# Three edits to a LayerNorm, attention and expert kernel: the order in which the QKV weights are loaded and used, and the queue that stores the output

## The reference

```python
def attn(x, Wq, Wk, Wv):                       # x: 8 x 4096 x 1024, per core 4096 x 1024
    q, k, v = x @ Wq.T, x @ Wk.T, x @ Wv.T     # each W 1024 x 1024
    scores = q @ k.T / sqrt(1024)              # causal
    return softmax(mask(scores)) @ v

def ffn(x, w1, b1, w2, b2, centroids, w_route):   # 8 experts, 1024 -> 512 -> 1024
    logits = normalize(x) @ normalize(centroids).T + x @ w_route.T
    gates = softmax over the top 2 of logits, 0 elsewhere
    h = gelu(x @ w1[e] + b1[e])
    return sum over e of gates[e] * (h @ w2[e] + b2[e])

x = x + attn(layernorm(x), Wq, Wk, Wv)
x = x + ffn(layernorm(x), ...)
```

## Time and profile before

| | us |
|---|---|
| median of 2 runs | 2174.48 (2174.03 to 2174.93) |
| the profiled execution | 2177.05 |
| its span, from the first to the last instruction of the slowest core (core 2) | 2175.5 |
| the other cores' spans | 2165.4 to 2172.9 |
| TensorE busy | 1889.7 (87%) |
| VectorE, ScalarE, GpSimd busy | 636.0, 496.0, 165.4 |

### The profile page before, as it was taken

One profiled execution on the slowest core, in us unless ns is written; L12 is line 12 of the kernel. 1 busy time (PEld: TensorE's weight loads), 2 busy tenths in 40 slices (PEclk: granted clock), 3 DMA queues, 4 the chain that ended last, 5 costly groups with the idle time before them and its releaser, 6 DMA issues.

```text
span 2175.5 us, 32734 instructions; the slowest of 8 cores (2165.4 to 2175.5 us)
## 1 busy us (share of the span) xinstructions
PE 1889.7 (87%) x12322; PEld 1131.7 (52%) x12448; DVE 636.0 (29%) x1606; ACT 496.0 (23%) x1140; POOL 165.4 (8%) x193
## 2 busy tenths in 40 slices
PE   2999999656688888989927899999999999999998
PEld 1777777323243443444415566555566665556663
DVE  2232322254633516050432122222212222221220
ACT  0333333211112021203003222212222222122220
POOL 1111111011100101010120000000000000000000
PEclk8999999777899999999968999999999999999999
DMA  9222221222321203030179511111001111110100
GB/s 177 62 66 78 69 78 50 81 93 92 114 71 49 92 25 117 1 102 16 54 152 171 104 40 49 49 49 49 26 34 40 49 49 49 49 47 13 49 30 39
DMA packets 41163, 142.80 MB, mean 66 GB/s; under 512 B 4114, under 2 KB 4114, under 8 KB 37938
## 3 DMA queue, kind: packets, MB, share of 16 engines
q0 software_dynamic: 25552, 73.42, 13.7%
q1 hardware_dynamic: 15458, 67.28, 9.7%
HBM read 113.44 MB, written 50.33 MB: 75 GB/s over the span
## 4 chain that ended last, share of the span: by engine, by line
PE 76%; DVE 9%; DMA 7%; issue 5%; ACT 1%; another core or an unknown queue 1%; POOL 1%; DVEq 0%; SPq 0%; ACTq 0%; POOLq 0%
PE ph L949 22%; PE pout L860 11%; PE psc L589 11%; PE pout L858 10%; PE pqk L395 9%; PE pv L356 5%; DMA x_scr<-x2b 3%; PE pctx L639 3%; PE pctx L641 3%; DVE x2b L662 2%; DMA arena<-w1s 2%; DVE stt L665 1%; DVE xr L666 1%; DMA xbuf<-x 1%
## 5 line engine op out<-in xcount | busy, mean ns | idle before, releaser
L949 PE MATMUL ph<-ln2Tg,arena 128*128 128x256 bf16 x4096 | 489.2, 285 | 35.5 <-DMA arena<-w1s 32.2
L949 PEld LDWEIGHTS ph<-ln2Tg,arena 128*128 128x128 bf16 x4096 | 386.8, 101 | 139.7 <-issue 42.1
L969 ACT ACTIVATE hT<-ph,b_s 128x256 bf16<-128x256 f32 x512 | 242.9, 474 | 754.0 <-PE ph L949 753.9
L860 PE MATMUL pout<-arena,hT 128*128 128x512 bf16 x1024 | 389.8, 381 | 11.2 <-DMA b_s<-b 8.7
L858 PE MATMUL pout<-arena,hT 128*128 128x512 bf16 x976 | 371.6, 381 | 0.0
L589 PE MATMUL psc<-qbuf,arena 128*128 128x512 bf16 x1127 | 269.0, 400 | 38.8 <-ACT probsT L602 29.3
L978 DVE TENSOR_TENSOR hT<-hT,gbc 128x256 bf16<-128x256 bf16 x512 | 149.8, 292 | 371.9 <-ACT hT L969 371.9
L395 PE MATMUL pqk<-xlnT,wqkv 128*128 128x256 bf16 x2048 | 233.1, 275 | 15.6 <-ACT arena L413 14.5
L639 PE MATMUL pctx<-arena,probsT 128*128 128x512 bf16 x504 | 201.4, 400 | 38.8 <-DVE x2b L662 38.8
L395 PEld LDWEIGHTS pqk<-xlnT,wqkv 128*128 128x128 bf16 x2048 | 200.8, 99 | 48.5 <-issue 20.0
L641 PE MATMUL pctx<-arena,probsT 128*128 128x512 bf16 x515 | 207.9, 404 | 20.4 <-DVE x2b L662 19.0
(11 more groups left out here) (95 smaller groups left out, 1052.0 us busy)
## 6 DMA issues: line engine op xcount, KB each, us to landing
xbuf<-x SPq DMA_DIRECT2D x32, 512.0 KB, 4.0
xr<-x SPq DMA_DIRECT2D x32, 512.0 KB, 3.6
x_scr<-x2b POOLq DMA_DIRECT2D x32, 512.0 KB, 3.7
x2g<-x_scr SPq DMA_DIRECT2D x16, 1024.0 KB, 5.8
out<-outsb POOLq DMA_DIRECT2D x32, 512.0 KB, 2.9
qt_scr<-qstage POOLq DMA_DIRECT2D x16, 512.0 KB, 3.8
qbuf<-qt_scr SPq DMA_DIRECT2D x8, 1024.0 KB, 6.9
ln2t_scr<-ln2Ts POOLq DMA_DIRECT2D x32, 256.0 KB, 3.2
```

The lines of the kernel that those rows point to most:

```text
L860: pe.matmul(pout[tl][:, 512:1024], lhs, arena[:, b + 512:b + 1024], start=(hc == 0), stop=False)
L949: mm = pe.matmul(ph[hc % 2][:, 0:256], arena[:, kd * 4096 + hc * 128: kd * 4096 + hc * 128 + 128], ln2Tg[:, gc % 2, kd, :], start=(kd == 0 ...
L969: s.activation(hT[:, gc % 2, hc, :], ph[hc % 2][:, 0:256], AF.Gelu, bias=b1s[:, hc:hc + 1]))
```

## The change

1. POOL waits for `cw` first and then loads Q, K, V in this order; before, K and V were loaded at once and Q after the wait.
2. SP waits for `cw` before its first load of x.
3. In the QK burst the first 8 units are Q and the last 8 are K (before, K first). The Q spill of a group waits for unit 7 instead of unit 15, and ScalarE's check that the spill before is done moves from unit 8 to unit 0.
4. The output tiles of stage C are stored from SP instead of POOL.

```diff
             def a1_gpsimd(g):
-                for i, wh in [(1, wkT_h), (2, wvT_h)]:
+                g.wait_ge(sVe.h, V["cw"])
+                for i, wh in enumerate([wqT_h, wkT_h, wvT_h]):
                     V["wqkv%d" % i] = sWt[i].inc(g.dma_start(
                         out=wqkv[:, i, :, :],
                         in_=wh.rearrange("(kd p) m -> p kd m", p=128)), 16)
-                g.wait_ge(sVe.h, V["cw"])
-                V["wqkv0"] = sWt[0].inc(g.dma_start(
-                    out=wqkv[:, 0, :, :],
-                    in_=wqT_h.rearrange("(kd p) m -> p kd m", p=128)), 16)
...
                 def a1_sync_t(sync, t=t):
+                    if t == 0:
+                        sync.wait_ge(sVe.h, V["cw"])
...
                 def a1_gp_g(gp, g=g):
                     gq, sub = g // 2, g % 2
-                    gp.wait_ge(sAc.h, qk_ev[(g, 15)])
+                    gp.wait_ge(sAc.h, qk_ev[(g, 7)])
...
-                    proj, m = 1 - u // 8, u % 8
+                    proj, m = u // 8, u % 8
...
                     def a1_sc_u(s, g=g, u=u, proj=proj, m=m):
                         s.wait_ge(sPe.h, qk_done[(g, u)])
-                        if u == 8 and g >= 1:
+                        if u == 0 and g >= 1:
                             s.wait_ge(sSp.h, qspill[g - 1])
...
-                    def c_gp_out(gp, t=t, tl=tl):
-                        gp.wait_ge(sVe.h, out_ev[t])
-                        out_st[t] = sF[t % 2].inc(gp.dma_start(
+                    def c_out_st(sync, t=t, tl=tl):
+                        sync.wait_ge(sVe.h, out_ev[t])
+                        out_st[t] = sF[t % 2].inc(sync.dma_start(
                             out=out_h[t * 128:(t + 1) * 128, :],
                             in_=outsb[:, tl, :]), 16)
-                    blk.gpsimd(c_gp_out)
+                    blk.sync(c_out_st)
```

## The result

The changed kernel is slower: 2226.36 us median (2216.22 to 2482.43, 11 runs) against 2176.14 for the kernel before in the same session (10 runs). The ratio is 1.0205, 95% interval 1.0192 to 1.0218; on 2174.5 us that is +44.6 us, where the prediction had +47 (2222, range 2199 to 2262). In some executions, of the kernel before too, two or more neighbouring cores take longer than the rest (by 10 to 30 us in the profiles of e1, e2 and e6, all of it ahead of the expert stage, and by over 250 us in the longest), and a time is that of the slowest core, so the ratios leave the longest executions out and single times can mislead. For this reason I also compare medians over the eight cores of a profiled execution, stage by stage.

The account below looks back on a forecast made before the run. It took TensorE, 87% busy, as bounding, so what lets it start at each seam matters. Wait 39, clock 7, start 1.5, end -0.5 summed to +47 us on 2174.5: 2222 us, range 2199 to 2262.

Parts of the forecast that it names:

- The wait per seam: Expert stage: TensorE waits 2.8 us for ln2Tg at each of 14 seams, 39 us in all (26 to 86).
- T0+5.1: ln2Tg's landing at a seam, counted from T0, SP's x2g issue before the change; bounds T0+4.11 and T0+8.41.
- second rival: Expert stage: x2g behind takes its share, ln2Tg lands after 7.9 us; 94 us in all, 2268; chance 0.15 with waits from 3.6.
- first rival: Expert stage: ln2Tg lands early, near the lower bound, since POOL's store is gone; +34 us, 2208; chance 0.2.
- The clock: Expert-stage bursts: restarting after a longer pause loses 0.5 us more per seam, +7 us in all (-6 to +13).
- bursts of 30.2 to 31 us: Expert stage: a sign of the forecast, the time each of the 14 hidden bursts would take.
- The start: Before the first stage ends: small loads gain, x and weights come later; +1.5 us in all (-1 to +12).
- just not late: Start: V, last of the weights, is in at 62.0 while TensorE takes it at 63.6.
- fourth rival: Start: V or x holds TensorE by 10 us or more, the forecast holding elsewhere; 2232 or more; chance 0.08.
- The end: Last output store: SP issues it 0.48 us earlier than POOL did, -0.5 us.
- 2 us before its burst: Expert stage, SP's queue: a sign of the forecast, where each ln2Tg issue would stand, 0.5 us behind a store.
- the bound: Whole kernel: two percent slower, 43.5 us (2218), about what a measurement can tell from no change.

Follow-up runs that it names:

- e1: The changed kernel with the output stores put back on POOL; ratio 1.0041 against the kernel before.
- e2: The kernel before with only the output stores moved to SP; ratio 1.0235.
- e6: The changed kernel with only the second store of each tail back on POOL; one run, 2202.1 us, median core span 2170.9.
- e4: The changed kernel with x2g loaded between the next tail's two stores, so nothing follows ln2Tg at the seam; median core span 2200.3 us.
- e8: The changed kernel with x2g issued before ln2Tg at the seam; shorter of two runs 2260.0 us, median core span 2249.8.
- e5: The changed kernel with the wait for the add kept ahead of ln2Tg, but ln2Tg issued before the second store; 2211.3 us.
- e3: The changed kernel, stores still on SP, with the next ln2Tg load issued ahead of both stores and x2g behind; ratio 1.0028.
- e9: The kernel before with K waiting only for the small loads, Q after cw, V last, and stores on SP behind ln2Tg; 2168.56 us, ratio 0.9943.
- e11: The kernel before with only x held for cw, K and V still loaded at once; median core span 2180.3 us.
- e7: The changed kernel with stores back on POOL and x not held for cw, weights still waiting; median core span 2173.9 us.

## Why the prediction was right, and where its terms were off

The place, the count and the direction were right: 14 waits on ln2Tg, at the seams of gc = 2 to 15, because SP's queue holds the load behind the wait for an add. The total was right to 3 us. But of the four terms of its sum the wait was 5 us and the start 1 us too small, the clock 8 and the end 3 us too large. That they cancelled is luck; the place and the count are not. By its own steps, in medians over the cores:

- **The wait per seam, 2.8 us, times 14 = 39.** Measured 3.34, times 14 = 46.8. The landing was right: the prediction had T0+5.1, and over the 28 seams of two cores ln2Tg landed on average 4.54 us after its issue, T0+5.08. The failed step is that it took the landing for the start of TensorE. In the same 28 seams the first matmul came 0.35 us after the landing, at T0+5.43: 5 us in all. A further 0.2 per seam is idle time that was there before (3.2 us in all, up to 0.3 each for the last gate copy); it makes the wait larger than the shift, which is 5.43 - 2.28 = 3.15. The 13 seams grew by 39.5 us, 3.04 each.
- **How T0+5.1 came about** was less sound than its value. The prediction priced the store ahead of the load and nothing behind. By e4 and e6 the store's bytes cost some 0.2 and x2g behind costs 0.75: the value was right, its reason in the main not. Its second rival named this mechanism and was turned down because ln2Tg would be the earlier of the two; x2g took its share all the same, but the landing came to 4.6 us and not 7.9. Its first rival, the lower bound, failed: with POOL's store gone the load still landed after 4.6, and only with x2g away (e4) after 3.8.
- **The clock, +0.5 per seam, +7 us.** Measured -0.06 per seam (30.07 us a burst against 30.13 as medians of the cores), -1 in all; e8 with the longest pauses has 29.9. The failed step is that two restarts, after 21.98 and 3.04 us, were read as a slope in the length of the pause. The mean loss at a restart in this stage was already 2.16 us, and it stays there. The prediction's own sign, bursts of 30.2 to 31 us, was missed from below by the median core.
- **The start, +1.5 us.** Measured +2.4 at A2 in the changed kernel (2.7 to 4.7 in the other profiles with the three edits) and +2.9 at the first ln2Tg issue. The failed step is that V would come "just not late". x landed after 4.2 and 6.3 us and not 8, and cw came at 10.8 and not 11.7, so the first x add ran at 17.7 (predicted near 20) and the QK burst began at 45.4 (near 48), earlier than before and not later (core 7), while V landed at 62.8. TensorE then waited 2.8 us for V in the median of the cores, which is over the 2 us that the prediction had named as a sign of being wrong, and on six of the eight cores the V burst took 8.3 to 8.8 us instead of 7.07; on cores 3 and 5 it took 7.07 after a wait as long. The fourth rival named this mechanism with a price of 10 us; it came with 2.8 us of wait.
- **The end, -0.5 us.** Measured -3.0 to -3.8: from the last store's issue to the end 7.0 us became 3.9. The prediction counted SP's earlier issue and left out what follows the store. The waits of SP's queue at the end, before and after (two kernels, a row each):

```profile
SPq L67 <- PEq L67: 3.8, 1, 3.8
```
```profile
SPq L67 <- PEq L67: 1.2, 1, 1.2
```

  This last wait is 3.8 us in the profiles where POOL issued all the stores (before, e1), 1.2 where SP did (the changed kernel, e2 to e5, e8), on every core, and 2.5 in e6, whose last store is POOL's. Why POOL's stores lengthen it is not shown. The remaining 0.5 is SP's earlier issue, as predicted, and 0.3 to 0.5 the landing of the last store, 2.6 us from SP and 2.9 to 3.1 from POOL (core 4).
- **Sum of what was measured:** 14 x 3.15 = 44.1, bursts -0.8, start +2.8, end -3.5, together 42.6; the median span grew by 42.2, the ratio says 44.6.
- **A sign that was misstated.** "2 us before its burst" for the ln2Tg issue doesn't fit the prediction's own landing at T0+5.1, which makes it 4.6; measured are 4.9.

Whether this is slower by over 2% the measurement itself hardly decides: the interval, 1.0192 to 1.0218, lies across the bound that the prediction put 4 us below its middle.

## What to carry to other kernels

An engine that issues DMAs is a queue of waits, and moving an instruction into it moves its wait ahead of everything behind; before a store is moved, list which loads stand behind it and how far ahead of their use they are now. If a store must share the queue, issue the next prefetch first (e3, e9). And a prediction of such a stall is a sum over landing, the step from landing to the waiting engine, and what was idle before; each has a row of its own.

## What the runs showed of the hardware that I had not expected

- A transfer of 1 MB issued 0.41 us behind a load of 512 KB in the same hardware queue slowed that load from 3.8 to 4.6 us (a store ahead in both), while a store of 512 KB issued 0.53 us ahead cost it only some 0.2 us (3.8 against the 3.6 of a lone load). Order of issue is not order of service., which the prediction read as such an order, show only that POOL's store started late beside x2g; why it did stays open.
- The Trainium skill ("DMA: Bandwidth & Descriptors", section "Queues, rings and completion order") says that on one engine descriptors are consumed in ring order. By that alone x2g, issued behind, would take nothing from ln2Tg, and it took 0.75 us (e4); with 1.5 MB ahead the load lands after 7.0 us (e8), which fits such an order better. Its turn-taking between queues agrees with e11, where x, issued at 16.5 us on SP, landed by 28.8, ahead of V's weights, issued at 2.6 on POOL and landed at 36.1.
- TensorE's loss at a restart did not grow with the pause: bursts of 30.13 us after 3.8 us of pause, 30.07 after 7, 29.9 after 10.
- Seven loads of at most 32 KB landed at 11.07 us beside two weight loads and at 6.28 us without them (at 6.2 to 6.9 on the cores of e7, where x is loaded beside them and the weights are not): 4.8 us of the start came from transfers of which only the small ones were urgent.
